# Layer of causal attention and two-wave mixing on one core: start reordered, slot transfers joined, order of work drawn up with other issue times

## What is computed

```python
x = x + attention(layernorm(x))      # rope on q and k, causal softmax, projection, bias
real = layernorm(x) @ cos(theta + theta_noise)
imag = layernorm(x) @ sin(phi + phi_noise)
x = x + sqrt(real * real + imag * imag)
```

## Time and profile before

| | |
|---|---|
| median of 3 runs | 2236.44 us (2230.28 to 2236.95) |
| profiled execution | 2240.03 us, its span 2238.3 us |
| TensorE busy | 2070.9 us, 93% |
| VectorE busy | 1601.9 us, 72% |
| ScalarE busy | 1296.1 us, 58% |
| GpSimd busy | 870.6 us, 39% |
| mean granted TensorE clock | 0.966 |
| DMA | 159.87 MB, 71 GB/s |

### The profile page before, as it was taken

One profiled execution on the slowest core, in us unless ns is written; L12 is line 12 of the kernel. 1 busy time (PEld: TensorE's weight loads), 2 busy tenths in 40 slices (PEclk: granted clock), 3 DMA queues, 4 the chain that ended last, 5 costly groups with the idle time before them and its releaser, 6 DMA issues.

```text
span 2238.3 us, 37555 instructions
## 1 busy us (share of the span) xinstructions
PE 2070.9 (93%) x12864; PEld 869.9 (39%) x12864; DVE 1601.9 (72%) x2868; ACT 1296.1 (58%) x1620; POOL 870.6 (39%) x1250
## 2 busy tenths in 40 slices
PE   4999999989999999999999999999999999999883
PEld 3333333334433344334443344334444344333331
DVE  4787777877778778787677767687777777778611
ACT  1346656655566565666567555665656565566571
POOL 4622324352444325343534434335244434432331
PEclk9889999999999999999999999999999999999996
DMA  5420222132212223222222222122122211221211
GB/s 159 115 62 23 73 61 88 42 103 60 82 55 80 61 61 88 65 84 87 75 70 77 72 65 79 58 75 84 56 77 71 81 60 52 73 72 32 78 58 43
DMA packets 119561, 159.87 MB, mean 71 GB/s; under 512 B 30662, under 2 KB 82246, under 8 KB 119110
## 3 DMA queue, kind: packets, MB, share of 16 engines
q1 hardware_dynamic: 118928, 155.22, 23.7%
q10 hardware_dynamic: 444, 2.26, 0.3%
HBM read 88.97 MB, written 50.86 MB: 62 GB/s over the span
## 4 chain that ended last, share of the span: by engine, by line
PE 62%; DMA 7%; DVE 7%; issue 7%; POOL 7%; ACT 5%; SPq 4%; POOLq 0%; DVEq 0%
PE banks L761 16%; PE banks L745 15%; PE banks L724 15%; PE banks L685 5%; DVE chunk_max L943 4%; PE banks L694 3%; ACT probs L831 3%; DMA rot<-raw 3%; PE banks L675 2%; PE banks L722 2%; DMA inverse<-inverses 2%; SPq L508 2%; PE banks L708 2%; POOL crossed L478 1%; SPq L525 1%
## 5 line engine op out<-in xcount | busy, mean ns | idle before, releaser
L943 DVE TENSOR_REDUCE chunk_max<-banks 128x1 f32<-128x512 f32 (+3 forms) x2240 | 1399.8, 671 | 433.6 <-PE banks L724 418.9
L831 ACT ACTIVATE probs<-banks 128x1024 f32<-128x1024 f32 (+3 forms) x1280 | 1074.7, 899 | 567.5 <-PE banks L745 543.1
L724 PE MATMUL banks<-stack_k,stack_q 96*128 96x512 bf16 (+3 forms) x2560 | 833.7, 357 | 35.3 <-DVE chunk_max L943 27.6
L745 PE MATMUL banks<-stack_q,stack_k 99*128 99x512 bf16 (+3 forms) x2560 | 694.4, 353 | 15.9 <-ACT probs L831 7.0
L761 PE MATMUL banks<-probs,v_one 128*17 128x512 f32 (+3 forms) x5120 | 539.0, 537 | 21.4 <-POOL probs L1078 20.2
L724 PEld LDWEIGHTS banks<-stack_k,stack_q 96*128 96x128 bf16 x2560 | 249.3, 99 | 406.2 <-DVE chunk_max L943 183.5
L745 PEld LDWEIGHTS banks<-stack_q,stack_k 99*128 99x128 bf16 x2560 | 220.9, 99 | 280.7 <-ACT probs L831 127.5
L1078 POOL TENSOR_SCALAR_AFFINE_SELECT probs<-probs 128x512 f32<-128x512 f32 x256 | 166.3, 655 | 314.1 <-ACT probs L831 307.8
L761 PEld LDWEIGHTS banks<-probs,v_one 128*17 128x17 f32 x5120 | 117.7, 97 | 303.0 <-issue 224.2
L722 PE MATMUL banks<-diag_mask,ident_bf 128*128 128x128 bf16 x1024 | 204.9, 225 | 12.7 <-DVE chunk_max L943 9.1
L722 PEld LDWEIGHTS banks<-diag_mask,ident_bf 128*128 128x128 bf16 x1024 | 100.3, 99 | 148.2 <-DVE chunk_max L943 75.3
(11 more groups left out here) (88 smaller groups left out, 1134.3 us busy)
## 6 DMA issues: line engine op xcount, KB each, us to landing
split<-parts SPq DMA_DIRECT2D x64, 384.0 KB, 2.6
stack_q<-split SPq DMA_DIRECT2D x384, 64.0 KB, 2.2
stack_k<-split SPq DMA_DIRECT2D x384, 64.0 KB, 2.2
rot<-raw SPq DMA_DIRECT2D x256, 64.0 KB, 2.0
sums<-o_raw SPq DMA_DIRECT2D x64, 256.0 KB, 2.1
xin<-x SPq DMA_DIRECT2D x16, 512.0 KB, 4.0
heads_t<-sums SPq DMA_DIRECT2D x28, 256.0 KB
mid<-x SPq DMA_DIRECT2D x14, 512.0 KB, 4.1
```

What stands on the lines that cost most here:

```text
L724: mm = nc.tensor.matmul(bank[:, n * wide:(n + 1) * wide], stack_q[u % 2][0:SPLIT_ROWS, t, h + n, j * P:(j + 1) * P], stack_k[u % 2][0:SPLI ...
L745: mm = nc.tensor.matmul(scores_bank[h][:, w0:SPAN], stack_k[u % 2][0:ROWS, j // SUB, h, (j % SUB) * P:(j % SUB + 1) * P], stack_q[u % 2][0 ...
L831: nc.scalar.activation(probs[:, g % PROBS, 2 * pair:2 * pair + 2, w0:SPAN], scores_pair[pair][:, :, w0:SPAN], ACT.Exp).then_inc(s_exp, 1)
L943: nc.vector.tensor_reduce(to, bank[:, 0:count * wide].rearrange("p (h n) -> p h n", h=count), AX.X, ALU.max).then_inc(s_emptied["DVE"], 1)
```

## The change

1. First loads: the weights of the first group come alone (`wqk[:, 0]`), the other three after the values' weights; the rotation tables come as the first 512 columns and then the rest; TensorE waits for each only where it is first used. The statistics of block 1 stand behind `normalise` of block 0 in the plan.
2. First rotation: of its four DMAs two are issued by SP and two by ScalarE, right after its copy.
3. Slot transfers: `SLOT_RUNS` makes six DMAs of a fetch where there were twelve: three, two and one slots at a time for each stack.
4. The plan: SP's durations and lags, `VALUES` 2 to 1, `SLACK` 0.2 to 0.4, a lag of 1.0 before the maxima are turned, and a small preference (`STICK`) for staying with one kind of work until `RUN` us are over.

```diff
+SLOT_RUNS = ((0, 0, 0, 3, True), (0, 3, 1, 2, True), (0, 5, 2, 1, True), (1, 0, 0, 3, False), (1, 3, 0, 2, False), (1, 5, 0, 1, True))
+HALVES = ((0, 32), (32, 0), (64, 96), (96, 64))
-VALUES = 2
+VALUES = 1
-LOADS = 2 * SLOTS * 16
+LOADS = len(SLOT_RUNS) * 16
-SLACK = 0.2
+SLACK = 0.4
+STICK = 0.05
+RUN = 4.0
+TURN_LAG = 1.0
...
-            job(("stats", n), "DVE", 2.1, at, [("xload", n), ("apply", n - 2), begun(at - SLACK)])
+            job(("stats", n), "DVE", 2.1, at, [("xload", n), ("apply", n - 2), *([("apply", 0)] if n == 1 else []), begun(at - SLACK)])
...
-            job(("rot", u, c), "SP", 0.3, at, [("out", ("qk", u, c, 1)), ("rope", *ago, 1)], 2.4)
+            job(("rot", u, c), "SP", 2.4 if i else 1.2, at, [("out", ("qk", u, c, 1)), ("rope", *ago, 1)], 1.8)
...
-            job(("fetch", u, c), "SP", 1.0, at, [("keep", u, c), ("scores", u - 2, NSTEP - 1, 1)], 4.0)
+            job(("fetch", u, c), "SP", 2.7, at, [("keep", u, c), ("scores", u - 2, NSTEP - 1, 1)], 2.2)
...
-            job(("split", u, c), "POOL", 1.3, at - 0.2, [("rowmax", u, c)])
+            job(("split", u, c), "POOL", 1.3, at - 0.2, [("rowmax", u, c)], TURN_LAG if u else None)
...
-            job(("rows", u, c), "SP", 0.3, at, [("out", ("turn", u, c))], 2.4)
+            job(("rows", u, c), "SP", 1.7, at, [("out", ("turn", u, c))], 1.8)
...
-            job(("inverse", n), "SP", 0.2, at, [("keepinv", n), ("add", prev), ("inverse", n - 1), *free], 2.5)
+            job(("inverse", n), "SP", 1.1, at, [("keepinv", n), ("add", prev), ("inverse", n - 1), *free], 4.5)
...
-            found.append((max(at, free[e]) + TURN_COST * change, jobs[name][2], name))
+            stick = STICK * change if free[e] - since < RUN else 0.0
+            found.append((max(at, free[e]) + TURN_COST * change, jobs[name][2] + stick, name))
...
-                    for at in range(0, P, P // 2):
-                        for own, other in ((at, at + 32), (at + 32, at)):
-                            sp.dma_start(rot[own:own + 32, i % 2, :], raw[other:other + 32, i % 2, :]).then_inc(s_rot[i % 2], 16)
+                    for own, other in HALVES[0:2] if i == 0 else HALVES:
+                        sp.dma_start(rot[own:own + 32, i % 2, :], raw[other:other + 32, i % 2, :]).then_inc(s_rot[i % 2], 16)
...
-                    for side, (tile, which) in enumerate(((stack_q, Q_PARTS), (stack_k, K_PARTS))):
-                        for slot, part in enumerate(which):
-                            rows = split[i % 2, part, side * P // 2:(side + 1) * P // 2, :]
-                            sp.dma_start(tile[u % 2][slot * HD:(slot + 1) * HD, c, :, :],
-                                         rows.rearrange("(d h) n -> d h n", h=HG)).then_inc(s_fetch[i % 2], 16)
+                    for side, slot, part, count, same in SLOT_RUNS:
+                        rows = split[i % 2, part:part + (1 if same else count), side * P // 2:(side + 1) * P // 2, :]
+                        if same:
+                            rows = rows.to_broadcast([count, P // 2, SPAN])
+                        tile = (stack_q, stack_k)[side][u % 2][slot * HD:(slot + count) * HD, c, :, :]
+                        sp.dma_start(tile.rearrange("p h n -> p (h n)"), rows.rearrange("m (d h) n -> m d (h n)", h=HG)).then_inc(s_fetch[i % 2], 16)
...
-                sp.dma_start(wqk[:, :, :, :], w_qk.rearrange("g p k n -> p g k n")).then_inc(s_wqk, 16)
+                sp.dma_start(wqk[:, 0, :, :], w_qk[0]).then_inc(s_wqk[0], 16)
                 load_block(1)
                 sp.dma_start(wv[:, :, :], w_v.rearrange("(k p) n -> p k n", p=P)).then_inc(s_wv, 16)
+                sp.dma_start(wqk[:, 1:GROUPS, :, :], w_qk[1:GROUPS].rearrange("g p k n -> p g k n")).then_inc(s_wqk[1], 16)
...
+                        if i == 0:
+                            ins.then_inc(s_emptied["ACT"], 1)
+                            emptied(act, item)
+                            for own, other in HALVES[2:4]:
+                                act.dma_start(rot[own:own + 32, 0, :], raw[other:other + 32, 0, :]).then_inc(s_rot[0], 16)
+                            return
```

More of the change, by code:

```diff
@@ L274, in plan @@
     held, bank, prior = [None] * RING, {}, {}
-    exact = None
+    exact, since = None, 0.0
     for name, n in left.items():
@@ L301, in plan @@
         if e == "PE":
+            if exact != (name[0] not in COARSE):
+                since = start
             exact = name[0] not in COARSE
@@ L411, in layer_kernel @@
         out_bank = psum[7]
-        s_wqk = sem("query_key_weights_loaded")
+        s_wqk = [sem(f"query_key_weights_loaded{n}") for n in range(2)]
         s_wv = sem("value_weights_loaded")
-        s_tables = sem("rotation_tables_loaded")
+        s_tables = [sem(f"rotation_tables_loaded{n}") for n in range(2)]
         s_corner = sem("diagonal_mask_loaded")
@@ L705, in project_values @@
                         bank_of(item)
+                        if q == 0 and c == 0:
+                            pe.wait_ge(s_wv, 16)
                     at = c * SPAN + j * P
@@ L849, in _ @@
                 act.dma_start(corner_t, corner).then_inc(s_corner, 16)
-                act.dma_start(cos_t[:, :], cosines).then_inc(s_tables, 16)
-                act.dma_start(sin_t[:, :], sines).then_inc(s_tables, 16)
+                for n, columns in enumerate((slice(0, SPAN), slice(SPAN, SEQ))):
+                    act.dma_start(cos_t[:, columns], cosines[:, columns]).then_inc(s_tables[n], 16)
+                    act.dma_start(sin_t[:, columns], sines[:, columns]).then_inc(s_tables[n], 16)
                 for n in range(2):
```

35 lines of the change are left out of this document (18 added, 17 removed).

## The result

| | before | changed |
|---|---|---|
| median of 4 runs each | 2233.36 us (2229.65 to 2236.95) | 2381.6 us (2379.18 to 2384.7) |
| ratio | | 1.0665 [1.0639, 1.0691] |
| profiled span | 2238.3 us | 2379.8 us |
| mean granted TensorE clock | 0.966 | 0.947 |

Slower by 6.7%, or 148 us. (One run of the kernel before, of those beside the last three experiments, took 3311.9 us at a granted clock of 0.566 and is left out of their ratios.) The sign was forecast, the size was not: the forecast was 2255 us, the range ended at 2300, and the rival with choking lanes was worked out to 2328. The page of the changed kernel begins with busy times that hardly differ from those of before on VectorE, ScalarE and GpSimd; TensorE is busy for 71 us more in a span that is 141.5 us longer (edges and half clock both lie in that busy time).

The account below looks back on a forecast made before the run. TensorE was taken as the bound, 1807 us of listed work plus some 430 of edges, waits and half clock. 74 - 29 - 24 - 14 + 20 - 8 = +19 us gave 2259 profiled, a median of 2255 us, range 2205 to 2300.

Parts of the forecast that it names:

- the rival with choking lanes: "The lanes choke": narrow joined loads hold up GpSimd and VectorE, then TensorE; +60 for +20, 2328 us; chance 0.18.
- part 3: SP's issue times and joined transfers: late-landing fetches delay rotations, denominators and inputs; +20 us, bounds -20 and +60.
- I take 13 us: Assumed time for a joined fetch to land, between 8.8 us (present fetch) and 15.7 us (one lane carrying 264 KB).
- the pair of rows with 8 lanes: Two 256 KB loads with outer dimension 8 taking 4.67 us, giving 0.055 us per KB a lane and 15.7 us landing.
- 7 x 6: Seven loads of denominators and a block's input behind a fetch, 6 us each, holding VectorE and GpSimd in order.
- Part 1: Values in one-step groups on TensorE: 319 more groups at 0.23 us of entry and exit, +74 us, bounds 60 and 80.
- the signs: Expected traces: TensorE busier by up to 74 us, exponential waits near 100, first maximum between 35 and 40 us.
- Part 2: TensorE waits given back by shorter groups: -29 us scores, -24 us maxima, -14 us turned maxima.
- the -29 of the sum: Less waiting of TensorE's scores for ScalarE's exponential: -29 us, bounds 0 and -45.
- the -24: Less waiting of TensorE's maxima for VectorE, 29% of 80 us: -24 us, bounds 0 and -45.
- Part 4: Reordered start: first maximum, then at 52.33 us, comes earlier, partly offset by slower landing; -8 us, bounds 0 and -17.
- The smoother feed wins: Shorter groups remove more than 86 us of TensorE's waits, outweighing the edges: -31, 2205 us; chance 0.33.

Follow-up runs that it names:

- the last three experiments: e13, e14 and e15, measured at 1.0638, 1.0147 and 0.9845 of the kernel before.
- e7: Kernel before with six joined loads interleaved over 16 partitions (all lanes), nothing else changed: 2228.64 us, 0.997.
- e10: e7 with the change's SP durations and lags in its plan; VALUES, SLACK and start as before: 2202.73 us, 0.9854.
- e15: e10 with the reordered start added: 2195.51 us, 0.9845.
- e5: Changed kernel with joined loads on all lanes, as e1, and VALUES = 2: 2215.49 us, 0.9924.
- e1: Changed kernel with each joined load's outermost dimension 16 rows instead of 3 or 2 slots: 2229.29 us, 0.9999.
- e2: Changed kernel with the fetch of before, twelve loads of 64 KB, under the changed plan: 2244.34 us, 1.0059.
- e4: Kernel before with the narrow joined loads alone, plan untouched: 2283.95 us, 1.0239.
- e14: e10 with the change's narrow joined loads, over 3 and 2: 2263.64 us, 1.0147.
- e13: Changed kernel with the seven loads of denominators directly behind a fetch on SP put directly before it: 2373.98 us, 1.0638.
- e6: Kernel before with VALUES = 1 alone, its plan drawn up again: 2304.99 us, 1.0321.
- e8: Kernel before with the reordered start alone (parts 1 and 2 of the change): 2230.18 us, 0.9989.

## Why the prediction was wrong, step by step

The runs put the change together in steps:

| kernel | what is added | ratio to before |
|---|---|---|
| e7 | six loads, all lanes | 0.997 |
| e10 | issue times in the plan | 0.9854 |
| e15 | reordered start | 0.9845 |
| e5 | `SLACK`, `STICK`, `TURN_LAG` | 0.9924 |
| e1 | values of one step | 0.9999 |
| the change | outermost dimension 3 and 2 | 1.0665 |

That e1 comes out even with before is a sum of large terms against each other: -7 for the six loads, -26 for the issue times, -2 for the start, +18 for `SLACK`, `STICK` and `TURN_LAG`, +17 for short groups. The prediction's terms other than part 3 add up to -1 us, which looks right and is so by luck: it had no term for the +18, and the -26 only inside the bound of part 3.

**The step that failed** is in part 3: "I put all of it at +20 us (bounds -20, with the present waits gone, and +60 ...)". The mechanism was named, its size was mis-taken: the narrow loads cost 149 us against six loads with all lanes, seven times the value and over twice the upper bound, and 135 us against the twelve loads of before in the same plan (e2). It failed in three places.
- The landing. "I take 13 us", between 8.8 and a worked-out 15.7. The timeline of the changed kernel has the first fetch issued at 34.15 and used at 51.34 us, 17.2 us:

```profile
34.15 2.02 SPq L536 DMA_DIRECT2D stack_q<-split  x3
...
51.34 0.29 PE L737 MATMUL banks<-diag_mask,ident_bf 128*128 128x128 bf16 x1 [7.95 <-DMA stack_k<-split]
```

  In e4 and e14, where the same narrow fetch comes first as well, it takes 15.2 and 15.6 us; with all lanes (e7 and e10) 7.7 and 7.9. The estimate from the pair of rows with 8 lanes was the right one, and taking less than it, toward the fetch of before, was the error: the row that was nearest in kind (a narrow outer dimension) should have gone ahead of the row that was nearest in name. The Trainium skill, "DMA: Bandwidth & Descriptors", section "Why a DMA increments its semaphore by 16 and not by 1", makes the number of engines the largest up to 16 that divides the slowest dimensions of both sides. The traces agree: 0.12 of 16 engines busy at 870 us is two, and with 16 in the outermost place the load lands in 3.3 us and 0.93 of the engines are busy.
- What stands behind. Only the 17 rotations and seven denominators and inputs that stand directly behind a fetch were counted. A narrow fetch holds up other transfers too that are issued in the dozen microseconds after it: rows of maxima (26.6 us on TensorE), and inverses, as e13 shows, where moving the one neighbour uncovers the next.
- The way to TensorE. "88.8 us of such waits on GpSimd reach TensorE as 20 now" was held against the rival, and most of the +20 was worked out on that path: rotation, GpSimd, mask. In the changed kernel it carries next to nothing: GpSimd waits 164.7 us for rotations, and TensorE's values 4.0 us for masks (20.2 before). What carries the loss is VectorE standing in its order until no bank is free, +70 us in TensorE's own waits against e1 (VectorE's waits for denominators and inverses are 80 us longer than there), which the prediction had at no more than 7 x 6 = 42; then the rows of the maxima, +25, for which it had nothing. (The bound doesn't follow from its own terms either: half of 17 x 6 and 7 x 6 is 72, or 52 less the present 20. Other slips, 74 for 73, 59 for 60 and 15.7 for 15.6 us, change nothing.) In the order of before (e4) the masks did carry, and there its bound held. Nor had it a price for what follows a long stop: in the two that were looked at TensorE worked at 1.2 GHz for some microseconds (567 to 570 us of the changed kernel at 0.50, 570 to 574 at 0.58).

**Part 1, +74 us: the price of an edge was right.** 636 groups, and in the changed kernel the entry is again 0.09 to 0.10 us and the exit 0.13 us, beside float32 neighbours too. e6 paid 72 us for 307 groups. The plan's own 0.1 us for a change of format would have given +22. That TensorE is 71 us busier in the changed kernel, near the "up to 74" of the signs, doesn't confirm it: with all lanes it is only 29 us busier than before (2099.9), and the other 42 came with the narrow loads.

**Part 2, -67 us, half right.** The exponential's wait is 60.1 us, below the "near 100" of the signs. By the prediction's own measure, less 0.21 us for each wait, it fell from 59 to 30, which is the -29 of the sum; "near 100" had left that measure out. The turned maxima's went from 32.1 to 10.0 as forecast. The maxima's, 258.8 us, rose to 380.6 even with all lanes (e1), with a time equal to before, and here the measure was at fault. It took off at most 0.43 us a wait, but 155 of the 507 were the loader idling behind a group of values, 0.77 us each and at almost no cost; in e1 these are 356. The other waits went from 140 to 98 us, less 0.21 each from 66 to 44: near the -24 after all. The count of places where four maxima stand close had foretold 29% less; it is a third. And what the waits gave back didn't pay for the edges in e6: net, short groups cost 72 us in the plan of before, 38 with the issue times and 17 in the whole changed plan; only the last is near the +7 of parts 1 and 2 together.

**Part 3 apart from the lanes.** A gain from issue times that are true was folded into "-20"; with sound lanes it is 26 us. The joined loads alone give up to 11, or 13 in a plan that counts on them.

**Part 4, -8 us, not there.** In the changed kernel the narrow fetch takes back what the start wins: the first maximum is at 51.34 us, 1 us earlier than the earlier trace rows, not "between 35 and 40". With all lanes it is at 42.8 us, and e8 and e15 show no gain at the end from that. VectorE's statistics of block 1 came no earlier (17.38 us, 17.66 before), since they wait for x.

**The rivals.** "The lanes choke" was the one, with its place, its mechanism and a chance of 0.18; "+60 in place of +20" was too small in it as well. "The smoother feed wins" was refuted as told (shorter groups cost time in each of the three plans with sound lanes), though a kernel at about its 2205 us exists, by the issue times alone.

## What to carry to other kernels

Before joining transfers, look at what stands outermost in the joined pattern: a count of 2 or 3 there made the first fetch take 15 to 17 us from issue to use, where it takes 7 to 9 with all lanes, and putting the 16 first cost one edited string and brought back 149 us. Price a slow transfer by all that its queue issues while it lasts, and ask by which engine the delay reaches the busiest one; do not scale a small stall's harmless share to one three times as long. A wait of the weight loader behind a group of values is no idle time of TensorE: look at TensorE's own rows before pricing it. For a static order, tell the planner the true time that issuing takes (1.2% here), and try each knob alone, since good and bad parts of one change hid each other (-26 and +18 us here).

## What was not expected of the hardware

- A DMA that has few lanes delays small ones that are issued behind it on the queue, though 14 of 16 DMA engines stand idle (0.12 busy at 870 to 877 us): 32 KB went from 2.2 to 8.6 us. Where the transfer just behind was moved ahead (e13), it landed in 2.3 us again.
- After a stop of 7.0 and one of 9.7 us TensorE ran at 0.50 for 3 us and at 0.93 and 0.58 for the 4 us that followed, so that the stall of 7 us cost nearly 9.
- With about the same work, the mean granted clock was 0.980 in e1, 0.967 in e5 and 0.947 in the changed kernel. In e1 318 more groups of values than in e5 made TensorE's busy time only 15 us longer.
- Issuing has a price on SP: three joined loads take 1.9 us there, four rotations 2.5 us, twelve loads of before 5.4 us (e8), and three rows of maxima once 3.46 us.
